# The two experts' weights of a routed feed-forward layer: an exponential and a reciprocal in place of a hyperbolic tangent

## The chip, the cores and the metric

The kernel runs on one core of one Trainium2 chip. The metric is the device time of one execution in microseconds (us).

The core has five engines with queues of their own: TensorE (PE in the profile, with its weight loads as PEld), VectorE (DVE), ScalarE (ACT), GpSimd (POOL) and SyncE (SP). Each runs its instructions in program order and waits on semaphores where it needs another's result.

## The reference, cut to what matters

The input is `x` of 16 images with 64 channels and 32 x 32 pixels. First comes a block of two binary convolutions on the channel-normalised input; its output is added to `x`. Then each of the 16384 pixels is a token of 64 values, which goes through a layer of 16 experts of which it uses two:

```python
logits = jnp.einsum('bsd,de->bse', x, gate_w) + gate_b
probs = jax.nn.softmax(logits, axis=-1)
top_probs, top_idx = jax.lax.top_k(probs, 2)
top_probs = top_probs / jnp.sum(top_probs, axis=-1, keepdims=True)
dispatch = jnp.sum(jax.nn.one_hot(top_idx, n_experts, dtype=x.dtype) * top_probs[..., None], axis=-2)
...
hidden = jax.nn.silu(h1) * h2
expert_out = jnp.einsum('bseh,eho->bseo', hidden, w3)
return jnp.einsum('bseo,bse->bso', expert_out, dispatch)
```

Only the two largest logits enter the two weights. With g as their difference, the weights are (1 + tanh(g/2))/2 for the first expert and (1 - tanh(g/2))/2 for the second.

## The kernel before

**Two halves.** The first half (to about 216 us of the profiled span) computes the convolutions and the routing; the second half computes the experts page by page.

**First half.** The images are taken in 8 pairs, so that 2 x 64 channels fill 128 partitions and a pair has 16 tiles of 128 tokens. All engines run one software pipeline over steps t = 0 to 11. In step t, pair t is normalised, pair t - 1 goes through its convolutions, pair t - 2 is normalised once more and gets its gate logits, pair t - 3 has its two experts chosen, and pair t - 4 gets its weights and the addresses of its rows. Each engine's order within a step is written out by hand:

- ScalarE (L640 to L677): `square2` and `copy2` of pair t - 2; `root(1)`, the logarithm and exponential for that pair's reciprocal root of the variance (L561 to L569); `conv1`; `sign`, `square` and `copy` of pair t; `channels`; `chosen_copy`; `relu`; `root(0)` of pair t; `wide`, which writes `rstd_wide`; `gap_tangent`, the tanh of half the gap (L621 to L625); in steps 3 and 4 a conversion of weights (`make_hi`).
- VectorE (L1458 to L1516): `weights` of pair t - 4 (L1293 to L1299); `first_choice`; `slots`, the rows' addresses; `second_choice`, which also makes the gap and, between its own instructions, `newton_sum` of pair t - 2 (L1189); `channels`; `score`; `places`; `conv2`; `residual`; the first root's steps; `find_line`; `line_parts`; `x_norm`. In step 8 the order of pages follows, in step 11 the list of experts of each page and then `rows_low`, which writes `xs_lo` (L1450).
- TensorE (L838 to L899): `variance(1)` of pair t - 2, for which it needs ScalarE's `square2` (L773); the first convolution; `turn_channels`; `center`; `gate` of pair t - 2 (L802), for which it needs VectorE's `newton_sum`; the second convolution (both at L757); `turn_chosen` (L811); `variance(0)`; `count`; `center2`; `norm` (L785), for which it needs `rstd_wide`; `rank` (L825 to L829).
- GpSimd scatters each pair's rows into pages by an indirect DMA for each tile, once `slots` of the pair is done.

**ScalarE's tables.** A function of ScalarE runs from a set of tables that is loaded by an instruction of its own (ACT_TABLE_LOAD in the profile). The code asks for the set that it names `natural_log_exp_and_others` at the start (L528) and in every `root(1)` (L563); where a function is not in the set that is loaded, a load appears ahead of it under that function's line, as at the tanh (L625) and the first silu (L691).

**The gap and the weights.** `gap` is 128 partitions x 16 tiles of float32. ScalarE waits for `gap_ready`, and from the second pair on for `weights_placed`, so that VectorE has read the last pair's values. VectorE's `weights` waits for `gap_done`. It holds the four experts of each token's line as +1, -1 or 0 in `by_x`, adds the tanh and multiplies by `by_x`: 1 + tanh, 1 - tanh or 0 goes into the row's payload; a factor of two is taken care of at the end. `then(...)` lets an instruction count up a semaphore (`route_link`), and `settled()` waits until all that was counted is done.

**Second half.** TensorE multiplies 147 pages of 128 rows by the weights of four experts each, with the silu on ScalarE, the products on VectorE and the results' scatter on GpSimd; at the end the results are turned back and added to the input.

Of the kernel before, what the change touches and what calls it, by code (L numbers as in the profile page):

```python
# [5 lines left out]
ALU = mybir.AluOpType  # L6
# [9 lines left out]
P = 128  # L16
# [12 lines left out]
PER_LINE = 4  # L29
# [21 lines left out]
def metaformer_kernel(nc, x, w1, gamma1, beta1, mean1, var1, w2, gamma2, beta2, mean2, var2,  # L51
# [33 lines left out]
    with ExitStack() as ctx:  # L85
        def sb(name, shape, dt):
            return ctx.enter_context(nc.sbuf_tensor(name, shape, dt))
# [79 lines left out]
        pick2 = sb("pick2", [P, TILES, E], F32)  # L167
        best = sb("best", [P, 4, TILES], F32)
        gap = sb("gap", [P, TILES], F32)
        gap_tanh = sb("gap_tanh", [P, TILES], F32)  # L170
        chosen = sb("chosen", [P, TILES, E], BF16)
        by_x = sb("by_x", [P, TILES, PER_LINE], F32)
# [353 lines left out]
        def _(act):  # L526
# [32 lines left out]


            def root(n, q):  # L561
                if n == 1:
                    act.preload_act_table_set("natural_log_exp_and_others")  # L563
                act.wait_ge((var_ready, var2_ready)[n], q + 1)
                if q:
                    act.wait_ge((rstd_ready, rstd2_ready)[n], q)
                act.activation(log_var[:, n, :], var_ps[n], ACT.Ln, bias=both_eps[:, n:n + 1]).then_inc(log_made[n], 1)
                act.wait_ge(log_made[n], q + 1)
                act.activation(guess[:, n, :], log_var[:, n, :], ACT.Exp, scale=-0.5).then_inc(guessed[n], 1)  # L569
# [51 lines left out]
            def gap_tangent(q):  # L621
                act.wait_ge(gap_ready, q + 1)
                if q:
                    act.wait_ge(weights_placed, q)
                act.activation(gap_tanh[:, :], gap[:, :], ACT.Tanh, scale=0.5).then_inc(gap_done, 1)  # L625

            def chosen_copy(q):
                act.wait_ge(chosen_turned, q + 1)
# [356 lines left out]
        def _(dve):  # L985
# [161 lines left out]
            def then(ins):  # L1147
                nonlocal links
                links += 1
                ins.then_inc(route_link, 1)  # L1150

            def settled(back=0):
                dve.wait_ge(route_link, links - back)
# [138 lines left out]

            def weights(q):  # L1293
                dve.wait_ge(gap_done, q + 1)
                settled()
                then(dve.tensor_tensor(sided[:, :, :], by_x[:, :, :], spread(gap_tanh[:, :], PER_LINE), ALU.add))
                settled()
                dve.tensor_tensor(payload[q % PAYLOADS][:, :, AT_WEIGHT:AT_WEIGHT + PER_LINE], sided[:, :, :],
                                  by_x[:, :, :], ALU.mult).then_inc(weights_placed, 1)  # L1299
# [304 lines left out]
```

## Time and profile before

| | |
|---|---|
| median of 3 runs | 535.71 us (534.81 to 540.6) |
| profiled execution | 537.69 us, span of the profile 536.0 us |
| mean granted TensorE clock | 0.932 of full speed |
| busy of the span: PE, DVE, ACT, POOL | 88%, 74%, 48%, 53% |
| instructions: DVE, ACT | 913, 462 |

The profile shows one execution. An engine's busy share is an average over both halves; which engine sets the time of a stretch is read from the chain of work that ended last, which is followed back from the last instruction: at each step to what released it, or to the instruction before it on its engine. The granted clock is what TensorE was given of its full 2.4 GHz; 0.50 is its level of 1.2 GHz.

### The profile page before, as it was taken

To read this page: it belongs to the slowest core of one execution; us is meant where nothing else is said; L and a number is where in the kernel's file an instruction comes from. 1 tells how busy PE (TensorE), PEld (TensorE's weight loads), DVE (VectorE), ACT (ScalarE), POOL (GpSimd) and SP (SyncE) were. 2 spreads that over 40 slices of the span, in tenths; PEclk is the share of its full clock that TensorE was granted. 3 is DMA by queue.
4 is the path that set the end of the run, shared out by engine and by line. 5 is a ranking of instruction groups with operands and counts; after the bars stand their busy time and mean duration, and the time that the engine had idled before them with its cause. 6 is when DMAs were issued, how large, how long until landed. Compare 5 with 4: busy or idle time off the path is not lost.

```text
span 536.0 us, 15131 instructions
## 1 busy us (share of the span) xinstructions
PE 474.1 (88%) x4774; PEld 417.1 (78%) x4774; DVE 397.3 (74%) x913; ACT 258.5 (48%) x462; POOL 281.5 (53%) x378
## 2 busy tenths in 40 slices
PE   6889999899998245899999999999999999999991
PEld 5457676767776223899999999999999999999981
DVE  5547777888989988777777677777778777777772
ACT  4557778988777212343443434343433434334320
POOL 4000006777777777777776444444544445455552
PEclk9779879999989756899999999999999999999996
DMA  7981011122000014431233222232422525310234
GB/s 265 325 149 40 1 41 35 53 71 65 30 32 30 28 32 92 87 71 30 62 81 68 56 43 54 49 93 50 121 64 49 130 48 149 75 37 16 74 109 157
DMA packets 62664, 41.03 MB, mean 77 GB/s; under 512 B 50003, under 2 KB 54318, under 8 KB 62080
## 3 DMA queue, kind: packets, MB, share of 16 engines
q1 hardware_dynamic: 52208, 23.84, 19.9%
q0 software_dynamic: 8800, 8.94, 5.2%
q10 hardware_dynamic: 1584, 7.29, 3.4%
q8 instruction: 45, 0.74, 0.6%
q14 instruction: 27, 0.22, 0.1%
HBM read 21.46 MB, written 19.19 MB: 76 GB/s over the span
## 4 chain that ended last, share of the span: by engine, by line
PE 78%; DVE 9%; issue 4%; DMA 3%; ACT 3%; SPq 1%; POOL 0%; POOLq 0%; DVEq 0%; ACTq 0%
PE turn L943 27%; PE up L928 12%; PE up L929 12%; PE up L757 8%; PE small L773 4%; PE small L906 3%; PE small L802 3%; DMA x_in<-in_x 3%; PE up L732 2%; PE turn L785 2%; PE lines L829 1%; PE up L743 1%; PE turn L796 1%; PE lines L950 1%; ACT rstd_wide L576 1%
## 5 line engine op out<-in xcount | busy, mean ns | idle before, releaser
L519 POOL DMA_INDIRECT results<-result,page_in x147 | 145.2, 988 | 129.7 <-ACT xc L691 102.4
L498 POOL DMA_INDIRECT pages<-payload,slot_int x128 | 130.4, 1018 | 108.6 <-DVE slot_int L1351 70.2
L691 ACT ACTIVATE xc<-up,gate_unscale 128x512 f32<-128x512 f32 x147 | 101.1, 687 | 175.5 <-PE up L929 143.6
L928 PE MATMUL up<-xs_hi,up_w 128*128 128x128 f16 x1176 | 148.7, 220 | 3.5 <-DVE hidden L1523 2.0
L929 PE MATMUL up<-xs_lo,up_w 128*128 128x128 f16 x1176 | 148.7, 220 | 0.0
L928 PEld LDWEIGHTS up<-xs_hi,up_w 128*128 x1176 | 123.4, 105 | 4.7 <-issue 4.0
L929 PEld LDWEIGHTS up<-xs_lo,up_w 128*128 x1176 | 115.7, 98 | 0.0
L1523 DVE SCALAR_TENSOR_TENSOR hidden<-up,hidden_scale,xc 128x512 f32<-128x512 f32 x74 | 55.4, 750 | 41.0 <-ACT xc L691 41.0
L943 PE MATMUL turn<-down_raw,hidden 128*128 x592 | 77.7, 275 | 3.4 <-issue 1.7
L943 PE MATMUL turn<-down_raw,sq 128*128 x584 | 78.1, 277 | 2.5 <-issue 0.7
L943 PEld LDWEIGHTS turn<-down_raw,sq 128*128 128x128 f32 x584 | 70.8, 191 | 10.3 <-issue 7.9
L943 PEld LDWEIGHTS turn<-down_raw,hidden 128*128 128x128 f32 x592 | 72.1, 192 | 8.4 <-issue 8.2
L1523 DVE SCALAR_TENSOR_TENSOR sq<-up,hidden_scale,xc 128x512 f32<-128x512 f32 x73 | 54.6, 748 | 24.0 <-ACT xc L691 22.9
L757 PE MATMUL up<-sign,conv_w 128*128 128x512 bf16 x192 | 48.9, 408 | 0.0
L757 PEld LDWEIGHTS up<-sign,conv_w 128*128 128x128 bf16 x192 | 19.8, 108 | 22.5 <-issue 4.7
L773 PE MATMUL small<-mean_col,sq 128*128 128x2 f32 x256 | 31.1, 252 | 5.8 <-ACT sq L553 3.4
L773 PEld LDWEIGHTS small<-mean_col,sq 128*128 128x128 f32 x256 | 30.5, 195 | 6.8 <-issue 3.5
L1534 DVE TENSOR_TENSOR branch<-turn,page_in 128x512 f32<-128x512 f32 (+1 forms) x38 | 25.9, 683 | 6.7 <-PE turn L943 6.6
L1534 DVE TENSOR_TENSOR rstd_wide<-turn,page_in 128x512 f32<-128x512 f32 x36 | 24.9, 691 | 4.7 <-PE turn L943 4.7
L684 ACT ACTIVATE xs_hi<-small 128x512 f16<-128x512 f32 (+1 forms) x37 | 22.0, 594 | 12.2 <-PE small L906 11.8
L1450 DVE SCALAR_TENSOR_TENSOR xs_lo<-small,xs_hi 128x512 f16<-128x512 f32 (+1 forms) x37 | 25.1, 678 | 0.9 <-ACT xs_hi L684 0.9
L802 PE MATMUL small<-gate_mat,xc 128*128 128x32 f32 x128 | 16.8, 288 | 9.9 <-DVE slack L1189 9.9
(234 smaller groups left out, 618.2 us busy)
## 6 DMA issues: line engine op xcount, KB each, us to landing
pages<-x ACTq DMA_DIRECT2D x4, 1332.0 KB, 10.8
page_in<-pages SPq DMA_DIRECT2D x147, 36.0 KB
page_in<-pages SPq DMA_DIRECT2D x147, 32.0 KB
x_in<-in_x SPq DMA_DIRECT2D x7, 512.0 KB, 3.5
out<-up_raw SPq DMA_DIRECT2D x5, 512.0 KB, 3.1
results<-result,page_in POOLq DMA_INDIRECT x147
up_raw<-in_L_ffn_w SPq DMA_DIRECT2D x4, 512.0 KB, 17.6
pages<-payload,slot_int POOLq DMA_INDIRECT x128
```

Source lines behind the costliest of these rows:

```text
L498: pool.indirect_dma_start(out=pages, out_offset=bass.IndirectOffsetOnAxis(ap=slot_int[q % PAYLOADS][:, t:t + 1], axis=0), in_=payload[q % ...
L519: pool.indirect_dma_start(out=results, out_offset=bass.IndirectOffsetOnAxis(ap=page_in[g % LOADS][:, k, D + AT_TOKEN:D + AT_TOKEN + 1].bit ...
L691: act.activation(act_s[n % 2], up[n % 2][:, 0:CW], ACT.Silu, scale=gate_unscale[:, 0:1])\
L757: last = pe.matmul(cv[c], conv_w[:, which, t, :], image[:, c * ROWS + i:(c + 1) * ROWS + i, j:j + W], start=(t == 0), stop=(t == len(TAPS) ...
L773: last = pe.matmul(var_ps[n][:, 2 * j:2 * j + 2], sq[:, j * P:(j + 1) * P], mean_col[:, :], start=True, stop=True)
L802: last = pe.matmul(gate_ps[:, j * 2 * E:(j + 1) * 2 * E], xc2[:, j * P:(j + 1) * P], gate_mat[:, :, :].rearrange("p a e -> p (a e)"), star ...
L928: pe.matmul(target, own, xs_hi[g % 2][:, at], start=True, stop=False)
L929: last = pe.matmul(target, own, xs_lo[g % 2][:, at], start=False, stop=True)
L943: last = pe.matmul(target, hidden[n % RING][:, at], whole[:, bass.ds(e, D)], start=True, stop=True)
L1450: dve.scalar_tensor_tensor(out=xs_lo[g % 2][:, 0:width], in0=small[:, 0:width], scalar=X_SCALE, in1=xs_hi[g % 2][:, 0:width], op0=ALU.mult ...
L1523: dve.scalar_tensor_tensor(out=hidden[n % RING], in0=up[n % 2][:, CW:HW], scalar=hidden_scale[:, 0:1], in1=act_s[n % 2], op0=ALU.mult, op1 ...
L1534: dve.tensor_tensor(weighed[g % 2][:, k:k + count, :, :], down_pair(m)[:, 0:count, :, :], weights.unsqueeze(3).to_broadcast([P, count, PER ...
```

## The change

With e = exp(-g), tanh(g/2) = (1 - e)/(1 + e). ScalarE computes e; VectorE adds 1, takes the reciprocal, and multiplies it by e - 1, which gives the negative of the tanh; the addition to `by_x` becomes a subtraction. There are two new tiles of 128 x 16 float32, the call for the table set in `root(1)` is dropped, and in `weights` the wait `settled()` ahead of the first instruction is dropped, with one behind each new instruction.

```diff
@@ -167,6 +167,8 @@
         gap = sb("gap", [P, TILES], F32)
+        gap_exp = sb("gap_exp", [P, TILES], F32)
+        gap_part = sb("gap_part", [P, TILES], F32)
         gap_tanh = sb("gap_tanh", [P, TILES], F32)
@@ -559,8 +561,6 @@
             def root(n, q):
-                if n == 1:
-                    act.preload_act_table_set("natural_log_exp_and_others")
                 act.wait_ge((var_ready, var2_ready)[n], q + 1)
@@ -622,7 +622,7 @@
                 act.wait_ge(gap_ready, q + 1)
                 if q:
                     act.wait_ge(weights_placed, q)
-                act.activation(gap_tanh[:, :], gap[:, :], ACT.Tanh, scale=0.5).then_inc(gap_done, 1)
+                act.activation(gap_exp[:, :], gap[:, :], ACT.Exp, scale=-1.0).then_inc(gap_done, 1)
@@ -1292,8 +1292,14 @@
             def weights(q):
                 dve.wait_ge(gap_done, q + 1)
-                settled()
-                then(dve.tensor_tensor(sided[:, :, :], by_x[:, :, :], spread(gap_tanh[:, :], PER_LINE), ALU.add))
+                then(dve.tensor_scalar(gap_part[:, :], gap_exp[:, :], 1.0, None, ALU.add))
+                settled()
+                then(dve.reciprocal(gap_part[:, :], gap_part[:, :]))
+                settled()
+                then(dve.scalar_tensor_tensor(out=gap_tanh[:, :], in0=gap_exp[:, :], scalar=-1.0, in1=gap_part[:, :],
+                                              op0=ALU.add, op1=ALU.mult))
+                settled()
+                then(dve.tensor_tensor(sided[:, :, :], by_x[:, :, :], spread(gap_tanh[:, :], PER_LINE), ALU.subtract))
                 settled()
```

## Rows read from the trace of the kernel before

**Rows 1.** The page's chain that ended last: share of the span by engine

```profile
PE 78%; DVE 9%; issue 4%; DMA 3%; ACT 3%; SPq 1%; POOL 0%; POOLq 0%; DVEq 0%; ACTq 0%
```

**Rows 2.** ScalarE's groups of instructions: line, operation, tile, count, busy us, mean ns

```profile
L563 ACT ACT_TABLE_LOAD x8 | 10.3, 1283 | 0.1
...
L625 ACT ACT_TABLE_LOAD x7 | 9.0, 1283 | 0.1
...
L625 ACT ACTIVATE gap_tanh<-gap 128x16 f32<-128x16 f32 x8 | 1.7, 215 | 0.1
```

**Rows 3.** ScalarE's timeline, 0 to 36 us: start, duration, line, operation, tile

```profile
1.24 1.28 ACT L528 ACT_TABLE_LOAD   x1 [1.24 <-PEq L1593]
...
13.80 0.27 ACT L567 ACTIVATE log_var<-small,both_eps 128x16 f32<-128x16 f32 x1 [1.69 <-PE small L773]
14.11 0.22 ACT L569 ACTIVATE guess<-log_var 128x16 f32<-128x16 f32 x1
...
34.97 1.28 ACT L563 ACT_TABLE_LOAD   x1
```

**Rows 4.** The chain in order of time, 93 to 98 us: start, duration

```profile
93.47 1.28 ACT L625
...
96.77 1.07 ACT sq L602 x2
```

**Rows 5.** TensorE's timeline, rounds 5 to 7; in brackets the idle time before it

```profile
95.15 1.34 PE L829 MATMUL lines<-line_hot,ones_b 128*128 128x320 bf16 x16
97.89 1.95 PE L773 MATMUL small<-mean_col,sq 128*128 128x2 f32 x16 [1.40 <-ACT sq L602]
...
104.94 1.87 PE L802 MATMUL small<-gate_mat,xc 128*128 128x32 f32 x16
...
116.83 1.93 PE L773 MATMUL small<-mean_col,sq 128*128 128x2 f32 x16
...
123.86 1.87 PE L802 MATMUL small<-gate_mat,xc 128*128 128x32 f32 x16
...
144.11 1.87 PE L802 MATMUL small<-gate_mat,xc 128*128 128x32 f32 x16
```

**Rows 6.** VectorE's groups of instructions, small shapes

```profile
L1194 DVE SCALAR_TENSOR_TENSOR rstd<-slack,guess 128x16 f32<-128x16 f32 x16 | 2.8, 173 | 0.3
...
L1122 DVE RECIPROCAL scales<-largest 128x3 f32<-128x3 f32 x1 | 0.2, 177 | 0.0
...
L1134 DVE RECIPROCAL unscale<-unscale 128x1 f32<-128x1 f32 x1 | 0.2, 165 | 0.0
```

**Rows 7.** VectorE timeline: a reciprocal, its successor, newton_sum in rounds 5 to 7

```profile
53.91 0.18 DVE L1122 RECIPROCAL scales<-largest 128x3 f32<-128x3 f32 x1
54.12 0.17 DVE L1123 TENSOR_SCALAR scales<-scales 128x3 f32<-128x3 f32 x1
...
102.89 0.17 DVE L1189 SCALAR_TENSOR_TENSOR slack<-small,slack 128x16 f32<-128x16 f32 x1
...
123.37 0.17 DVE L1189 SCALAR_TENSOR_TENSOR slack<-small,slack 128x16 f32<-128x16 f32 x1
...
142.87 0.17 DVE L1189 SCALAR_TENSOR_TENSOR slack<-small,slack 128x16 f32<-128x16 f32 x1
```

**Rows 8.** The chain in order of time, rounds 8 and 9

```profile
155.26 0.23 DVE sided L1296
...
163.45 1.97 PE small L802 x16
165.42 2.64 PE up L757 x12
...
177.41 0.24 DVE sided L1296
```

**Rows 9.** VectorE timeline at the first page of the second half; brackets: idle

```profile
211.02 0.69 DVE L1450 SCALAR_TENSOR_TENSOR xs_lo<-small,xs_hi 128x512 f16<-128x512 f32 x1 [0.92 <-ACT xs_hi L684]
```

**Rows 10.** Two us by engine: PE, PEld, DVE, ACT, POOL, granted clock, DMA, GB/s

```profile
132.00:134.00 2.00, 1.61 (x8) 1.61 (x9) 0.53 (x2) 1.98 (x3) 1.70 (x2) 0.50 0.74 270
```

## The prediction

> **What bounds the kernel now.** I read the chain that ended last first: TensorE carries 78% of the span, VectorE 9%, ScalarE 3% [rows 1]. The change touches only the first half (up to about 216 us), in the loop of steps t = 0 to 11 that I call rounds, so the question is which engine that chain runs through where ScalarE's table loads and VectorE's `weights` stand. I therefore read ScalarE's groups, to see what is removed; the chain around the one load that lies on it; TensorE's and VectorE's timelines of rounds 5 to 7; and the chain of rounds 8 to 11. The reader is to see three stretches. Up to round 7 the chain is TensorE's own work, and ScalarE makes it wait for a load once, in round 5 [rows 4, 5]. From `weights` of round 8 on, VectorE is the chain: `sided` stands on it in rounds 8 and 9 [rows 8], and so it goes on in round 10. In round 11 VectorE waits again, for ScalarE's `xs_hi` [rows 9]. Behind that the second half is TensorE's and is not touched, so a delay of the first half moves its end by the same amount.
>
> **What the change removes.** Fifteen table loads of 1283 ns: 8 asked for in `root` and 7 placed before the tanh, 19.2 us of ScalarE's time in all [rows 2]. No pause hangs on them: the idle time ahead of the 8 tanh is 0.1 us together [rows 2]. The exponential takes the place of the tanh at the same price: 0.22 us for the same shape, against 215 ns [rows 2, 3]. That no new load appears is read from the start: the table loaded at 1.24 us serves a logarithm at 13.80 and an exponential at 14.11, and the next load comes at 34.97 and is asked for by the code [rows 3]. So one set has all that the loop needs once the tanh is gone. The load for the silu stays.
>
> What of the 19.2 us lies on the chain? In 14 of 15 cases ScalarE catches up before TensorE needs it. In round 6, for instance, TensorE starts `variance` at 116.83 with no idle time ahead of it [rows 5], although two loads lie around it. These 14 I cost at nothing; TensorE's own matmuls are the cover. The exception is round 5. TensorE ends `rank` at 95.15 + 1.34 = 96.49 and waits until 97.89 for ScalarE's squares, which end at 96.77 + 1.07 = 97.84 behind the load of 93.47 and a weight conversion [rows 4, 5]. Without the load the squares end at 96.56 and TensorE starts at about 96.61: **-1.28 us**, bounded from below by nothing and from above by the wait of 1.40.
>
> [...]
>
> **What it adds.** Three VectorE instructions in each `weights`, in a chain of dependences. An add and a scalar_tensor_tensor of 128x16: 173 ns each by the nearest row [rows 6]. A reciprocal of 128x16 is not in the trace: 165 ns at one column and 177 at three [rows 6] make 165 as the lower bound and, at 6 ns a column, 165 + 15 x 6 = 255 as the upper; I take 210. From the end of one to a dependent start goes 0.03 us (53.91 + 0.18 to 54.12) [rows 7]. Together 0.20 + 0.24 + 0.20, so **0.65 us** a round, 0.60 to 0.70.
>
> [...]
>
> Behind `weights` on VectorE stand the choice of experts, `slots`, and `newton_sum`, for which TensorE's `gate` (L802) waits. Round by round:
> - Round 4 is covered by the clock-slowed TensorE work that VectorE waits for; I cost it at nothing, and at 0.65 if that cover is gone.
> - Round 5: `newton_sum` ends at 103.06 [rows 7], with the addition 103.71. `gate` would start at 104.94 - 1.28 = 103.66 [rows 5]. **+0.1**: the gain of 1.28 just fits.
> - Round 6: `newton_sum` ends at 123.54, with the addition 124.19, but TensorE was ready at 123.86 [rows 5, 7]. **+0.35**: here TensorE waits anew, and all behind `gate` is later.
> - Round 7: 143.04 + 0.65 = 143.69 before 144.11 [rows 5, 7]: nothing, because TensorE had lost time at its lower clock just before [rows 10]. At full clock it would cost as in round 6.
> - Rounds 8, 9 and 10: on the chain [rows 8], nothing covers it: 3 x 0.65 = **+1.95**.
> - Round 11: the wait of 0.92 us ahead of `xs_lo` [rows 9] swallows it.
>
> **Sum:** -1.28 + 0.1 + 0.35 + 1.95 = +1.1 us. The profiled execution took 537.69 us (span 536.0), 2 us above the median of the runs; the change is small against both, so I add it to the median: 535.71 + 1.1 = **536.8 us**. The bounds of the prices: lowest -1.40 + 0 + 0.2 + 1.8 = +0.6; highest, with no gain in round 5, rounds 4, 6 and 7 uncovered and 0.70 each, 0.7 x 6 = +4.2, and that is 539.9.
>
> **Rivals.**
> - *The table loads are on the path throughout.* [...] If each of the 15 loads delayed the chain, their removal would give 15 x 1.283 = 19.2 us, against 1.95 to 4.2 added: about 519 to 520. For it: ScalarE loses these 19.2 us for certain. Against it: ScalarE is 3% of the chain, and one load stands on it [rows 1, 4]. Chance 0.05.
> - *The lower clock reaches round 8* (ends on the other side). TensorE's granted clock drops to 0.50, the 1.2 GHz level, in places: in 132 to 134 us, where TensorE was busy 1.61 of 2.00 us [rows 10]. The addition makes TensorE wait longer for `newton_sum` ahead of `gate` of round 8. If the clock falls there, `gate` and the convolution behind it, 1.97 + 2.64 = 4.6 us on the chain [rows 8], take twice as long: 536.8 + 4.6 = 541.4. It decides only if the whole stretch is slow. For it: such a drop already followed a partly idle stretch. Against it: VectorE's chain, not TensorE's clock, sets rounds 9 to 11. Chance 0.09.
> - *VectorE binds in every round.* Six or seven rounds at 0.65 and no gain: 539.6 to 540.3. Against it: the covers counted above. Chance 0.06.
> - *The change doesn't do what it says:* logarithm and exponential get different sets and each `root` pays two loads. For the 8 roots on the chain that is 8 x 2 x 1.283 = 20.5 us: 557. Against it: rows 3 show both under one load. Chance 0.02.
>
> **How the numbers follow.** The forecast, with the clock's drops moved by at most a stretch either way, has 0.78. Such a stretch of some 3 us at half speed costs about 1.5 us, estimated from the halved clock [rows 10]; two less or two more of them make 536.8 -/+ 3. With the bound of 539.9 and the case of VectorE in every round, the range is 533.5 to 540.5. A measurement of this kernel tells about 1%, 5.4 us, from no change. Faster by more than that needs the first rival: 0.05. Slower needs the clock, the wrong sets, or both costs together: 0.11. Within 1%: 0.84.
>
> **What would show it.** Right: one table load at the start and one before the first silu, 19 us less busy time on ScalarE, no idle TensorE ahead of round 5's `variance`, an idle TensorE of some 0.3 us ahead of round 6's `gate`, `weights` longer by 0.65 us, and the first `xs_lo` about 1 us later. Wrong: further table loads; a reciprocal much above 255 ns; `xs_lo` earlier than 211.02; another count of stretches at the lower clock; or a second half that is not as long as before.

## The result and the profile after

| | before | after |
|---|---|---|
| median | 538.22 us (20 runs, 534.52 to 544.54) | 540.66 us (20 runs, 537.9 to 543.78) |
| profiled execution, span | 537.69 us, 536.0 us | 539.03 us, 537.3 us |
| mean granted TensorE clock | 0.932 | 0.932 |

The ratio after to before is 1.0049 [1.0028, 1.0070], so +2.6 us [+1.5, +3.8]. (Ratios leave disturbed executions out, so they need not be the quotient of two medians.) The 20 runs of before also put its median 2.5 us above the 535.71 us of the three runs that the prediction started from. 540.66 us lies 3.9 us above the forecast of 536.8 and 0.16 us above the range.

The page of after, first the busy time of the engines (share of the span, instructions), then the chain that ended last. VectorE has 11% of the chain where before it had 9% [rows 1]:

```profile
PE 475.3 (88%) x4774; PEld 416.6 (78%) x4774; DVE 402.0 (75%) x937; ACT 238.9 (44%) x447; POOL 279.8 (52%) x378
...
PE 82%; DVE 11%; issue 3%; ACT 2%; DMA 1%; POOL 1%; POOLq 0%; DVEq 0%; SPq 0%
```

ScalarE's groups of after (line, operation, tile, count, busy us, mean ns). Of the fifteen loads of [rows 2] none is left; the load at the start and the one for the silu stay. The exponential takes 201 ns where the tanh took 215:

```profile
L625 ACT ACTIVATE gap_exp<-gap 128x16 f32<-128x16 f32 x8 | 1.6, 201 | 0.0
L530 ACT ACT_TABLE_LOAD x1 | 1.3, 1283 | 1.3 <-PEq L1599 1.3
L691 ACT ACT_TABLE_LOAD x1 | 1.3, 1283 | 0.0
```

VectorE's groups of the three new instructions, and its timeline where they run in round 4 (start, duration). From the start of the first to the start of `sided` it is 91.74 - 91.05 = 0.69 us:

```profile
L1297 DVE RECIPROCAL gap_part<-gap_part 128x16 f32<-128x16 f32 x8 | 2.0, 253 | 0.3
...
L1299 DVE SCALAR_TENSOR_TENSOR gap_tanh<-gap_exp,gap_part 128x16 f32<-128x16 f32 x8 | 1.4, 174 | 0.3
...
L1295 DVE TENSOR_SCALAR gap_part<-gap_exp 128x16 f32<-128x16 f32 x8 | 1.3, 166 | 0.0
```

```profile
91.05 0.16 DVE L1295 TENSOR_SCALAR gap_part<-gap_exp 128x16 f32<-128x16 f32 x1
91.24 0.25 DVE L1297 RECIPROCAL gap_part<-gap_part 128x16 f32<-128x16 f32 x1
91.53 0.17 DVE L1299 SCALAR_TENSOR_TENSOR gap_tanh<-gap_exp,gap_part 128x16 f32<-128x16 f32 x1
91.74 0.23 DVE L1302 TENSOR_TENSOR sided<-by_x,gap_tanh 128x64 f32<-128x64 f32 x1
```

So what the change does to the two engines is what was predicted. The time went elsewhere, and TensorE's timeline shows where. After, round 4 to round 5: the wait of 1.40 us ahead of `variance` [rows 5] is gone (93.36 has no bracket), but behind the wait for `rstd_wide` the `norm` takes 1.97 us and the four products behind it 1.84:

```profile
88.43 1.97 PE L785 MATMUL turn<-ident,rstd_wide 128*128 128x128 f32 x8 [0.91 <-ACT rstd_wide L576]
90.19 1.84 PE L743 MATMUL up<-x,center_mat 128*128 128x256 f32 x4
...
93.36 1.93 PE L773 MATMUL small<-mean_col,sq 128*128 128x2 f32 x16
```

The same place in round 5 of before, with the same wait, at full clock:

```profile
113.47 1.18 PE L785 MATMUL turn<-ident,rstd_wide 128*128 128x128 f32 x8 [0.91 <-ACT rstd_wide L576]
114.48 1.03 PE L743 MATMUL up<-x,center_mat 128*128 128x256 f32 x4
```

Four stretches of after around that `norm` in rounds 4 to 7 (us, busy time by engine, then the granted clock, here 0.57 to 0.73; 0.50 in 109 to 111 us alone):

```profile
88.00:92.00 4.00, 3.57 (x13) 3.02 (x14) 2.23 (x8) 3.37 (x5) 3.06 (x4) 0.57 0.44 154
108.00:112.00 4.00, 3.09 (x13) 2.81 (x13) 2.25 (x7) 1.74 (x4) 3.09 (x4) 0.61 0.54 168
128.00:132.00 4.00, 3.09 (x13) 2.52 (x12) 2.30 (x7) 1.74 (x4) 2.95 (x4) 0.67 0.50 162
148.00:152.00 4.00, 3.10 (x13) 2.62 (x14) 2.54 (x10) 1.97 (x6) 3.08 (x4) 0.73 0.10 31
```

After's rounds are 20.48 us long there, from each `norm` to the next; before, where the `norm` ran at full clock in rounds 4 and 5 (1.18 us), the round from 113.47 to 132.39 took 18.92.

And in round 8, TensorE's timeline of after: the gate waits 1.16 us for `newton_sum`, and the convolution behind it takes 4.46 us, where in before the same twelve products took 2.81 us (2.64 on the chain, [rows 8]) behind a wait of 0.54 (granted clock 0.51 in 164 to 167 us of after, 1.00 in 165.4 to 168 us of before):

```profile
161.42 1.97 PE L802 MATMUL small<-gate_mat,xc 128*128 128x32 f32 x16 [1.16 <-DVE slack L1189]
163.23 4.46 PE L757 MATMUL up<-sign,conv_w 128*128 128x512 bf16 x12
```

Put together for the two profiled executions, each mark's start in us:

| mark | before | after | difference |
|---|---|---|---|
| `norm` of round 3 | 71.17 | 69.11 | -2.06 |
| `norm` of round 4 | 92.98 | 88.43 | -4.55 |
| `norm` of round 5 | 113.47 | 108.92 | -4.55 |
| `norm` of round 7 | 152.64 | 149.88 | -2.76 |
| `gate` of round 8 | 163.45 | 161.42 | -2.03 |
| `gate` of round 9 | 185.61 | 185.89 | +0.28 |
| first `xs_lo` | 211.02 | 211.99 | +0.97 |

The first -2.06 is not the change's: it was there at `gate` of round 2 (42.73 against 40.69), because before's `norm` at 29.95 ran at the lower clock (1.97 us, where after's at 29.27 took 1.17), ahead of the first load that the change removes (34.97, [rows 3]). The `xs_lo` row of after answers to [rows 9]; its wait for ScalarE has shrunk from 0.92 to 0.43 us:

```profile
211.99 0.69 DVE L1456 SCALAR_TENSOR_TENSOR xs_lo<-small,xs_hi 128x512 f16<-128x512 f32 x1 [0.43 <-ACT xs_hi L684]
```

From the first `hidden` to the end of the span both take about the same: 536.0 - 215.78 = 320.2 and 537.3 - 216.75 = 320.6 us. So the first `xs_lo` came 1 us later, as predicted, but out of other terms. Between rounds 3 and 4 after gained 2.5 us, where before ran at the lower clock; its stretch behind the `norm` of round 3 (the granted clock is the 0.50 behind the engines):

```profile
72.00:76.00 4.00, 4.00 (x16) 2.87 (x15) 3.35 (x9) 3.99 (x6) 0.00 (x0) 0.50 0.13 49
```

Between rounds 4 and 5 it gained nothing: the wait of 1.40 us is gone and the slow stretch behind `norm` took its place. By round 7 it gave back 1.8 us, and from there to `xs_lo` it lost 0.73 + 2.31 + 0.69 = 3.7 us instead of 1.95.

### The profile page after: what moved, and what is told of

It is laid out like the page before. It is cut to its first block, busy times and chain, and to the rows that moved or that the text cites. A ratio compares the mean times of both kernels' runs of the same rounds, so it can differ in the third digit from the quotient of the medians.

```text
span 537.3 us, 15132 instructions
## 1 busy us (share of the span) xinstructions
PE 475.3 (88%) x4774; PEld 416.6 (78%) x4774; DVE 402.0 (75%) x937; ACT 238.9 (44%) x447; POOL 279.8 (52%) x378
## 4 chain that ended last, share of the span: by engine, by line
PE 82%; DVE 11%; issue 3%; ACT 2%; DMA 1%; POOL 1%; POOLq 0%; DVEq 0%; SPq 0%
PE turn L943 27%; PE up L928 12%; PE up L929 12%; PE up L757 9%; PE small L773 5%; PE small L906 3%; PE small L802 3%; PE up L732 3%; PE turn L785 2%; PE lines L829 1%; PE up L743 1%; PE turn L796 1%; PE lines L950 1%; ACT rstd_wide L576 1%; DVE up_w L1142 1%
## 5 line engine op out<-in xcount | busy, mean ns | idle before, releaser
L500 POOL DMA_INDIRECT pages<-payload,slot_int x128 | 128.6, 1005 | 109.7 <-DVE slot_int L1357 68.1
L757 PE MATMUL up<-sign,conv_w 128*128 128x512 bf16 x192 | 51.4, 423 | 0.0
L757 PEld LDWEIGHTS up<-sign,conv_w 128*128 128x128 bf16 x192 | 20.5, 112 | 24.6 <-issue 8.6
L684 ACT ACTIVATE xs_hi<-small 128x512 f16<-128x512 f32 (+1 forms) x37 | 22.0, 594 | 12.1 <-PE small L906 11.8
L802 PEld LDWEIGHTS small<-gate_mat,xc 128*128 128x128 f32 x128 | 16.9, 209 | 12.3 <-DVE slack L1189 12.1
```

The lines of the kernel that those rows point to most:

```text
L500: pool.indirect_dma_start(out=pages, out_offset=bass.IndirectOffsetOnAxis(ap=slot_int[q % PAYLOADS][:, t:t + 1], axis=0), in_=payload[q % ...
L684: act.activation(xs_hi[g % 2][:, 0:width], small[:, 0:width], ACT.Copy, scale=X_SCALE)\
L757: last = pe.matmul(cv[c], conv_w[:, which, t, :], image[:, c * ROWS + i:(c + 1) * ROWS + i, j:j + W], start=(t == 0), stop=(t == len(TAPS) ...
L802: last = pe.matmul(gate_ps[:, j * 2 * E:(j + 1) * 2 * E], xc2[:, j * P:(j + 1) * P], gate_mat[:, :, :].rearrange("p a e -> p (a e)"), star ...
```

## The experiments

Two theories went in. P: the prices of the prediction, the lower clock comes by chance. C: TensorE's waits, which the change moves, decide where its clock falls. Changes in us are the ratio times the median of before in the same set (539.55, then 541.25, then 539.22).

### The loads alone

`loads_only` is the changed kernel without its three VectorE instructions:

```diff
-                then(dve.tensor_scalar(gap_part[:, :], gap_exp[:, :], 1.0, None, ALU.add))
-                settled()
-                then(dve.reciprocal(gap_part[:, :], gap_part[:, :]))
-                settled()
-                then(dve.scalar_tensor_tensor(out=gap_tanh[:, :], in0=gap_exp[:, :], scalar=-1.0, in1=gap_part[:, :],
-                                              op0=ALU.add, op1=ALU.mult))
-                settled()
-                then(dve.tensor_tensor(sided[:, :, :], by_x[:, :, :], spread(gap_tanh[:, :], PER_LINE), ALU.subtract))
+                settled()
+                then(dve.tensor_tensor(sided[:, :, :], by_x[:, :, :], spread(gap_exp[:, :], PER_LINE), ALU.subtract))
```

> The changed kernel without its three new VectorE instructions: the exponential goes into the weights as it is, so the weights are wrong ones and only the time is of use. What is left of the change is that 15 table loads are gone. Theory P (the terms of the prediction's sum hold, and the stretches of TensorE's lower clock move about by chance): -1.3 us against the kernel before, 0.24% faster. Theory C (without the loads, rounds 5 to 8 each have a stretch at the lower clock and take 20.5 us, so what the loads gave back is lost there): no gain, 0 to +1.5 us, and the profile shows a stretch at 1.2 GHz behind the wait for rstd_wide in all four rounds.

Measured: 537.21 us, ratio 0.9941 [0.9903, 0.9979], -3.2 us. The gain is larger than the one load of 1.28 us that P found on the chain, but its interval, -5.2 to -1.1 us, just reaches that. C was wrong on the time. Its mechanism is in the profile, though: the `norm` of rounds 5, 6 and 7 takes 1.97 us (at 111.40, 131.54 and 151.86; the granted clock was 0.50 in 111.4 to 113.4 us), that of round 4 1.18. This execution took 537.45 us, about as long as the profiled one of before (537.69), so the two profiles don't show where the 3.2 us come from.

### The three instructions alone

`trio_only` is the kernel before, with its tanh and its loads, and three instructions of the same shapes whose result nobody reads:

```diff
-                settled()
+                then(dve.tensor_scalar(gap_part[:, :], gap_tanh[:, :], 3.0, None, ALU.add))
+                settled()
+                then(dve.reciprocal(gap_part[:, :], gap_part[:, :]))
+                settled()
+                then(dve.scalar_tensor_tensor(out=gap_exp[:, :], in0=gap_tanh[:, :], scalar=-1.0, in1=gap_part[:, :],
+                                              op0=ALU.add, op1=ALU.mult))
+                settled()
                 then(dve.tensor_tensor(sided[:, :, :], by_x[:, :, :], spread(gap_tanh[:, :], PER_LINE), ALU.add))
```

> The kernel before with its tanh and all its table loads, and three VectorE instructions of the same kinds and shapes as the new ones ahead of sided in weights; their result is used by nothing. Theory P: +2.3 us (0.35 in round 6, 3 x 0.65 in rounds 8 to 10), 0.43% slower; with the loads' -1.3 this makes the +1.0 of the sum. Theory C: the same +2.3 us, and it is nearly all that the whole change costs (+2.6). If the three instructions cost more than their durations say, +3.5 us or more.

Measured: 540.98 us, ratio 1.0047 [1.0004, 1.0091], +2.5 us [+0.2, +4.9]. The size is as both theories expected. TensorE's timeline shows two things: in round 6 the gate waits 0.26 us for `newton_sum`, as the prediction had for that round (+0.35), and at 143.10 in round 7 again; and in round 8 the wait of 1.12 us is again followed by a convolution of 4.46 us:

```profile
123.65 1.97 PE L804 MATMUL small<-gate_mat,xc 128*128 128x32 f32 x16 [0.26 <-DVE slack L1191]
...
163.22 1.97 PE L804 MATMUL small<-gate_mat,xc 128*128 128x32 f32 x16 [1.12 <-DVE slack L1191]
165.03 4.46 PE L759 MATMUL up<-sign,conv_w 128*128 128x512 bf16 x12
```

### The three instructions from round 8 on

`trio_late` runs them only where the prediction has them on the chain:

```diff
+                if q >= 4:
                     then(dve.tensor_scalar(gap_part[:, :], gap_exp[:, :], 1.0, None, ALU.add))
 ...
+                else:
+                    settled()
+                    then(dve.tensor_tensor(sided[:, :, :], by_x[:, :, :], spread(gap_exp[:, :], PER_LINE), ALU.subtract))
```

> The changed kernel with its three new VectorE instructions in the last four of the eight pairs only (rounds 8 to 11); in the first four the exponential goes into the weights as it is, so half of the weights are wrong ones. Theory P: -1.3 + 1.95 = +0.7 us. Theory C: +1.95 to +3.5 us, the same as the whole change, since rounds 4 to 7 cost nothing by either account but for 0.35.

Measured: 539.11 us, ratio 1.0003 [0.9970, 1.0037], +0.2 us. Against before that is nearer to P's number than to C's, but the gain from the loads, which P had put at 1.3 us and C at nothing, had come out larger than either. Against `loads_only`, which differs by these four rounds alone, it is +3.4 us by the ratios and 1.9 us by the two medians (539.11 and 537.21), so the times don't decide between 1.95 us and more. The two profiles, which both have the `norm` of round 7 at the lower clock, show more: `norm` of round 7 to `gate` of round 8 is 11.49 against 10.82 us, that gate to the next 24.44 against 22.10, and on to `xs_lo` 26.10 against 25.40: 0.67 + 2.34 + 0.70 = 3.7 us, as from before to after. In `loads_only` the gate of round 8 waits 0.52 us and the convolution stays at full clock (1.00 in 164.5 to 167 us):

```profile
162.68 1.97 PE L802 MATMUL small<-gate_mat,xc 128*128 128x32 f32 x16 [0.52 <-DVE slack L1189]
164.49 2.81 PE L757 MATMUL up<-sign,conv_w 128*128 128x512 bf16 x12
```

So in these profiles the three instructions cost about 0.7 us in each of these rounds, and in round 8 1.6 us more by TensorE's clock.

### No loads and nothing more on VectorE

tanh(g/2) = 2/(1 + e) - 1, and 1/(1 + e) = exp(-ln(1 + e)). The one table load at the start serves both the logarithm and the exponential [rows 3], so `on_scalar` lets ScalarE compute the whole and folds the factors into the two VectorE instructions that are there anyway:

```diff
-                act.activation(gap_exp[:, :], gap[:, :], ACT.Exp, scale=-1.0).then_inc(gap_done, 1)
+                act.activation(gap_exp[:, :], gap[:, :], ACT.Exp, scale=-1.0).then_inc(gap_step, 1)
+                act.wait_ge(gap_step, 2 * q + 1)
+                act.activation(gap_log[:, :], gap_exp[:, :], ACT.Ln, bias=all_one[:, 0:1]).then_inc(gap_step, 1)
+                act.wait_ge(gap_step, 2 * q + 2)
+                act.activation(gap_tanh[:, :], gap_log[:, :], ACT.Exp, scale=-1.0).then_inc(gap_done, 1)
@@ weights
+                then(dve.scalar_tensor_tensor(out=sided[:, :, :], in0=spread(gap_tanh[:, :], PER_LINE), scalar=2.0,
+                                              in1=by_x[:, :, :], op0=ALU.mult, op1=ALU.add))
+                settled()
+                dve.scalar_tensor_tensor(out=payload[q % PAYLOADS][:, :, AT_WEIGHT:AT_WEIGHT + PER_LINE],
+                                         in0=sided[:, :, :], scalar=-1.0, in1=by_x[:, :, :],
+                                         op0=ALU.add, op1=ALU.mult).then_inc(weights_placed, 1)
```

> All on ScalarE, in the one table set that stays: e = exp(-g), then ln(1 + e), then exp of the negative of that, which is the first expert's weight; VectorE's weights has two instructions as before the change, of another kind. ScalarE's table loads are gone and 0.55 us a round are added to it. Theory P: -0.8 to -1.3 us against the kernel before. Theory C: 0 to +1.5 us. Both: 2.3 us less than the changed kernel or a little more.

Measured: 535.37 us, ratio 0.9939 [0.9908, 0.9969], -3.3 us: faster than before. ScalarE's groups show the price, 0.72 us a round where the tanh took 0.22:

```profile
L627 ACT ACTIVATE gap_log<-gap_exp,all_one 128x16 f32<-128x16 f32 x8 | 2.5, 308 | 0.3
L629 ACT ACTIVATE gap_tanh<-gap_log 128x16 f32<-128x16 f32 x8 | 1.7, 216 | 0.2
L625 ACT ACTIVATE gap_exp<-gap 128x16 f32<-128x16 f32 x8 | 1.6, 200 | 0.0
```

In its profile the `norm` of rounds 4 to 7 runs at full clock each time (1.18 us), and from round 5 on the rounds are 18.92 us long. But ScalarE has little room in the two rounds in which it also converts weights. TensorE waits 0.56 us for its squares in rounds 4 and 5; in round 4 the clock falls behind that wait (0.59 in 80 to 83 us), and from `norm` to `norm` it is 94.68 - 73.39 = 21.29 us:

```profile
77.46 2.15 PE L777 MATMUL small<-mean_col,sq 128*128 128x2 f32 x16 [0.56 <-ACT sq L602]
79.47 4.24 PE L761 MATMUL up<-sign,conv_w 128*128 128x512 bf16 x12
```

And the gate of round 8 waits 1.24 us, and the clock falls there too (0.57 in 164 to 168 us):

```profile
162.25 1.97 PE L806 MATMUL small<-gate_mat,xc 128*128 128x32 f32 x16 [1.24 <-DVE slack L1193]
164.05 4.46 PE L761 MATMUL up<-sign,conv_w 128*128 128x512 bf16 x12
```

### TensorE kept busy in the wait for `rstd_wide`

`after_again` is the changed kernel once more. `after_fill`, `before_fill` and `on_scalar_fill` are the changed kernel, the kernel before and `on_scalar`, each with four products that nobody reads in the wait ahead of the first half of `norm`, in rounds 1 to 7:

```diff
-                pe.wait_ge(widened, CH * q + c + 1)
                 if q == 1:
 ...
+                if q and c == 0:
+                    for _ in range(4):
+                        pe.matmul(turn[0][:, :], ident_b[:, :],
+                                  conv_w[:, 0, 0:4, :].rearrange("p t o -> p (t o)"), start=True, stop=True)
+                pe.wait_ge(widened, CH * q + c + 1)
                 for t in range(TPC):
```

> The changed kernel once more, unaltered, on the same chip as the three kernels with filled waits. By all theories +1.1 to +2.6 us against the kernel before; theory C adds that its profile again has a stretch at 1.2 GHz behind the wait for rstd_wide in most of rounds 4 to 8 and that its mean granted clock is lower than that of the kernel before.

> The changed kernel with four matrix products of 128x512 in bf16 in TensorE's wait for rstd_wide (0.91 us a round), into a bank that the transposes behind them overwrite; nothing reads their result. Theory C (the changed kernel loses 1 us and more a round to stretches at 1.2 GHz that begin behind that wait): with the wait filled TensorE keeps 2.4 GHz, rounds 5 to 7 take 19.2 to 19.5 us in place of 20.5, and the kernel is 3 to 4 us faster than the changed kernel, so 0.5 to 2 us faster than the kernel before. Theory P (the stretches come by chance, and not from that wait): as the changed kernel, within 0.5 us.

> The kernel before with the same four products in the same wait. Theory C: 2 to 4 us faster than the kernel before, which has two such stretches in rounds 7 and 8 of its profile at 1.3 to 1.5 us each. Compared with the changed kernel that has its wait filled, the difference is then what the prediction's sum says without the clock: 1.1 us. Theory P: as the kernel before.

> The kernel with all three functions on ScalarE (on_scalar), and the same four products in the same wait. Its profile without them has no stretch at 1.2 GHz in rounds 4 to 8, so both theories expect little: theory C 0 to 1.5 us less than on_scalar, since other executions of it have such stretches; theory P the same as on_scalar, 3 to 4 us below the kernel before.

| | median, us | ratio to before | us |
|---|---|---|---|
| `after_again` | 540.15 | 0.9994 [0.9965, 1.0023] | -0.3 |
| `after_fill` | 533.18 | 0.9878 [0.9821, 0.9936] | -6.6 |
| `before_fill` | 535.12 | 0.9880 [0.9824, 0.9937] | -6.5 |
| `on_scalar_fill` | 535.08 | 0.9893 [0.9844, 0.9942] | -5.8 |

In the changed kernel and in the kernel before, this is the largest effect of a single edit in the study, and it comes from work that computes nothing; it is more than C had forecast (3 to 4 and 2 to 4 us). `on_scalar` gains less by it: its ratio was 0.9939 without the products and is 0.9893 with them, in another set, and the medians are alike (535.37 and 535.08). With the wait filled the three ways to compute the weights can't be told apart: their changes lie within 0.8 us, each with some 3 us either side. TensorE's timeline of `after_fill`, round 5: the four products take 1.03 us where TensorE waited 0.91, `norm` runs in 1.24 us instead of 1.97, and from round 4 to round 7 each round takes 19.33 us instead of 20.48:

```profile
108.15 1.03 PE L784 MATMUL turn<-conv_w,ident_b 128*128 128x512 bf16 x4
109.22 1.24 PE L789 MATMUL turn<-ident,rstd_wide 128*128 128x128 f32 x8
110.30 1.03 PE L743 MATMUL up<-x,center_mat 128*128 128x256 f32 x4
```

With this cover gone, the next place shows: the gate of round 8 now waits 1.92 us, and the clock falls behind it as before the fill (0.54 in 161 to 164 us):

```profile
158.68 1.97 PE L806 MATMUL small<-gate_mat,xc 128*128 128x32 f32 x16 [1.92 <-DVE slack L1193]
160.49 4.45 PE L757 MATMUL up<-sign,conv_w 128*128 128x512 bf16 x12
```

`before_fill` shows what went with a table load on the chain. Its profiled execution is one of its two longest (540.7 us; the other four took 532.5 to 536.6 at mean granted clocks of 0.938 to 0.947 against 0.930, and where their clock fell isn't seen). ScalarE's timeline, and under it TensorE's: the load of 69.62 and the conversion `up_w` stand ahead of the squares; TensorE waits 1.34 us for them, and behind the wait `variance` takes 2.86 us and the convolution 5.16, against 1.93 and 2.80 in before (77.42 and 79.21); the granted clock was 0.50 in 77 to 81 us. That is 1.34 + 0.93 + 2.36 = 4.6 us, in round 4 (the wait at 74.04) and once more behind the wait of 1.33 us at 97.80:

```profile
69.62 1.28 ACT L625 ACT_TABLE_LOAD   x1
70.91 0.22 ACT L625 ACTIVATE gap_tanh<-gap 128x16 f32<-128x16 f32 x1
71.03 1.99 ACT L636 ACTIVATE up_w<-up_raw,scales 128x2048 f16<-128x2048 f32 x1
72.93 1.06 ACT L602 ACTIVATE sq<-up 128x512 f32<-128x512 f32 x2
```

```profile
71.36 1.34 PE L833 MATMUL lines<-line_hot,ones_b 128*128 128x320 bf16 x16
74.04 2.86 PE L773 MATMUL small<-mean_col,sq 128*128 128x2 f32 x16 [1.34 <-ACT sq L602]
76.77 5.16 PE L757 MATMUL up<-sign,conv_w 128*128 128x512 bf16 x12
```

So in this one execution a load of 1.28 us goes with a loss of 4.6 us, where the clock falls behind the wait. Where it doesn't, the loss stays near the wait, as in round 5 of before [rows 5] and in `before_hold`, one of the kernels below. That has the same two waits, at full clock (1.00 in 72 to 100 us); its rounds with them are 20.49 us long each (`norm` at 66.95, 87.44 and 107.93), the two behind them 18.98 and 18.99 (126.91 and 145.90), so a load is worth 1.5 us there:

```profile
71.85 1.95 PE L773 MATMUL small<-mean_col,sq 128*128 128x2 f32 x16 [1.33 <-ACT sq L602]
...
92.34 1.95 PE L773 MATMUL small<-mean_col,sq 128*128 128x2 f32 x16 [1.34 <-ACT sq L602]
```

### TensorE kept busy ahead of round 8, and in rounds 9 and 10

`after_gate8` is the changed kernel with five products only ahead of the gate of round 8. The three `_hold` kernels are the three `_fill` kernels with these five, and with 40 more in the long waits ahead of the gate of round 9 and ahead of `turn_chosen` of round 10:

```diff
+                if q == PAIRS - 2:
+                    fill(up[0][:, 0:CW], 5)
+                if q == PAIRS - 1:
+                    fill(up[0][:, 0:CW], 40)
                 pe.wait_ge(var2_read, q + 1)
@@ turn_chosen
+                if q == PAIRS - 1:
+                    fill(up[0][:, 0:CW], 40)
                 pe.wait_ge(chosen_ready, q + 1)
```

> The changed kernel with five matrix products of 128x512 in bf16 at one place only: TensorE's wait for newton_sum ahead of gate of round 8 (1.1 to 1.2 us in the changed kernel), into a bank that is free by then; nothing reads their result. Theory C (the longer wait there lets the clock fall in the convolution behind it, which took 4.46 us in place of 2.81): the convolution takes 2.8 us again and the kernel is 1.6 us faster than the changed kernel. Theory P: the products lie in a wait and change nothing, within 0.5 us.

> The changed kernel with products in all of TensorE's long waits of the first half from round 1 on: four ahead of norm, five ahead of gate of round 8, forty ahead of gate of round 9 and forty ahead of turn_chosen of round 10, so that TensorE keeps 2.4 GHz. Theory C: the kernel with only the wait ahead of norm filled, less 1.6 us in round 8, 1.8 us at gate of round 9 (3.62 to 1.87) and some 2 us at rank and the first page's transposes: 5 us less than that one, 11 to 12 us less than the changed kernel. Theory P: as the changed kernel.

> The kernel before with the same products in the same waits. Theory C: 9 to 12 us less than the kernel before; its rounds 4 and 5 keep TensorE's wait for the squares behind a table load and, in some executions, a lower clock behind that. With the clock held, the terms of the prediction's sum give 0.3 to 1.1 us less than the changed kernel with the same products; if the loads let the clock fall in rounds 4 and 5, it is slower than that one by up to 5 us.

> The three functions on ScalarE and the same products in the same waits. Theory C: the fastest of all: 2.5 to 3.5 us less than the changed kernel with the same products (0.34 a round in rounds 5 to 8, 0.65 in rounds 9 and 10), 13 to 15 us less than the kernel before. Theory P: as on_scalar.

| | median, us | ratio to before | us |
|---|---|---|---|
| `after_gate8` | 539.41 | 1.0020 [0.9991, 1.0050] | +1.1 |
| `after_hold` | 532.88 | 0.9879 [0.9824, 0.9935] | -6.5 |
| `before_hold` | 534.98 | 0.9901 [0.9849, 0.9953] | -5.3 |
| `on_scalar_hold` | 529.71 | 0.9840 [0.9782, 0.9898] | -8.6 |

In its own place `after_gate8` does what it is for: TensorE's timeline of round 8 has no wait and the convolution at full clock (1.00 in 165.8 to 168.5 us).

```profile
162.89 1.03 PE L801 MATMUL up<-conv_w,ident_b 128*128 128x512 bf16 x4
164.00 1.97 PE L809 MATMUL small<-gate_mat,xc 128*128 128x32 f32 x16
165.81 2.81 PE L757 MATMUL up<-sign,conv_w 128*128 128x512 bf16 x12
```

With it the wait of round 8 can be set against the length of that stretch in eight profiles without a fill at `norm`:

| kernel | idle ahead of the gate | convolution behind it | gate of round 8 to gate of round 9 |
|---|---|---|---|
| `loads_only` | 0.52 | 2.81 | 22.10 |
| before | 0.54 | 2.81 | 22.16 |
| `after_gate8` | 0, filled | 2.81 | 22.85 |
| `on_scalar` | 1.24 | 4.46 | 23.76 |
| `trio_late` | 1.10 | 4.46 | 24.44 |
| `trio_only` | 1.12 | 4.46 | 24.47 |
| `after_again` | 1.13 | 4.46 | 24.47 |
| after | 1.16 | 4.46 | 24.47 |

The two costs come apart: with the three instructions the stretch is 24.47 - 23.76 = 0.71 us longer at the same clock, and with the fall of the clock 24.47 - 22.85 = 1.62 us longer with the same instructions. In this place the wait of 1.1 us and more comes with the fall each time, the waits of 0.52 and 0.54 us and the filled one don't. That is no rule for other places: in `on_scalar` the fall came behind the wait of 0.56 us ahead of the squares.

The time of the whole kernel doesn't show these 1.6 us: +1.1 us against before, where `after_again` had -0.3 in another set, with intervals that overlap. In the profile of `after_gate8` the `norm` of rounds 1 and 2 ran at the lower clock (at 50.09 for 1.97 us, where after has 1.18) and its `norm` of round 7 starts at 152.46, 2.6 us later than after's. Why its early rounds are slower than after's is left open.

`after_hold` brings the gate of round 9 back to full clock, 1.97 us for 3.62 in after (1.00 in 181.6 to 183.6 us, where after has 0.50 in 185.9 to 189.5), and shows no `norm` above 1.24 us from round 1 on:

```profile
171.62 8.58 PE L805 MATMUL up<-conv_w,ident_b 128*128 128x512 bf16 x39
181.64 1.97 PE L815 MATMUL small<-gate_mat,xc 128*128 128x32 f32 x16 [1.44 <-DVE slack L1204]
```

From gate to gate it is 181.64 - 158.80 = 22.84 us, and the first `hidden` starts at 210.38, 3.8 us earlier than in `after_fill`. In the medians of six runs each that isn't seen: 532.88 against 533.18. `on_scalar_hold` is the fastest kernel, 8.6 us below before [5.5, 11.8]; in its profile the first `hidden` starts at 204.50, against 215.78 in before. C had asked for more of all three: 11 to 12 us below the changed kernel, where `after_hold` is 6.5 us below `after_gate8` in the same set, and 9 to 12 and 13 to 15 us below before, where `before_hold` and `on_scalar_hold` have 5.3 and 8.6.

## Why the prediction missed

**In short.** Of the 3.9 us above the forecast, 2.5 are the base (535.71 us, where 20 runs have a median of 538.22), and the rest is the change, +2.6 us where the sum had +1.1. The step of the sum that failed is the price of a wait of TensorE: it was set at the wait's own length, and the lower clock that can follow was left out of the sum, as a rival in round 8 and as chance elsewhere. In rounds 8 to 10, where the prediction had 3 x 0.65 = 1.95 us, the profiles show 3.7, of which 1.65 are the clock's in round 8.

**Loads removed: right.** Fifteen loads are gone, no other came, ScalarE is busy 19.6 us less. The rival that had each of them on the path (519 to 520 us) fell: without the three instructions, `loads_only` gained 3.2 of 19.2 us. The other 16.0 us didn't show in the time; in round 6 of before, for instance, TensorE starts `variance` at 116.83 with no wait [rows 5], with loads at 113.95 and 117.42. No pause shows at a load: in `before_fill` the tanh starts at 70.91, right behind the load that ended at 69.62 + 1.28 = 70.90, and in before ScalarE was idle for 0.1 us together ahead of the seven loads at the tanh, and for 0.1 us ahead of the eight tanh [rows 2].

**The term of -1.28 was read from one execution.** The prediction found the one load on the chain, priced it at its own length with the wait of 1.40 us as the upper bound, and cost the other 14 at nothing, with TensorE's own matmuls as the cover. Measured alone, the loads were worth -3.2 us [-5.2, -1.1], which isn't clear of -1.28. Two steps are too short. One of the 14, the load of round 4, was covered in before's profile by the lower clock alone (72 to 76 us); in `before_hold`, at full clock, TensorE waits 1.33 us for it, and the two rounds are 1.5 us longer each, 3.0 us together. And the wait is no upper bound: in the profile of `before_fill` a wait of 1.34 us was followed by 3.3 us lost at the lower clock. How often either happens in before isn't shown: its profiled execution has one such wait, at full clock.

**The price of the three instructions: right,** at the upper end. The reciprocal took 253 ns, where the rows gave 165 to 255 (the 255 an estimate at 6 ns a column) and the prediction took 210; the three together 0.69 us, and 0.71 by the table of round 8, against 0.65 (0.60 to 0.70).

**Rounds 5 to 7: right in mechanism, hidden by the clock.** The predicted idle TensorE ahead of round 6's `gate` isn't there after (120.87 has no bracket): TensorE had lost more than that at the lower clock in the `norm` of round 5 (1.97 us for 1.18), as the prediction had argued for round 7 alone. Where the clock stayed up, in `trio_only` (`norm` of rounds 5 and 6 in 1.18 us), the gate waited 0.26 us in round 6 and 0.26 in round 7. With the wait filled the whole round tells the same: 19.33 us from `norm` to `norm` in `after_fill` and `after_hold`, against 18.98 in rounds 6 and 7 of `before_hold`, so 0.35 us, the price that the prediction had for round 6.

**Rounds 8 to 10: the term of +1.95 was mis-sized, at 3.7 us.** VectorE is the chain there, as predicted, and 0.73 + 0.66 + 0.69 of it are the three instructions (the middle one is 2.31 less the clock's 1.65). The rest is the rival of the lower clock in round 8, which had a chance of 0.09 and a price of 4.6 us. It came, by the mechanism that the prediction named, the longer wait for `newton_sum` ahead of the gate. It took the convolution alone (4.46 against 2.81 us) and left the gate at 1.97, so its price was 1.65. The argument against it, that VectorE's chain sets these rounds, failed: what VectorE does next waits for that convolution. Its timeline shows it idle for 0.55 and 1.22 us ahead of the two halves of `residual` in after (L1166, at 165.75 and 167.72), each time for TensorE's L757, and for 0 and 0.21 us in before. The sum of 3.7 us is that of two pairs of profiles (before and after, `loads_only` and `trio_late`); the medians don't confirm it by themselves.

**The clock in rounds 4 to 7 was left out of the sum.** The prediction let its stretches move by one "either way" and so gave them a mean of nothing. After has one in the `norm` of every round from 4 to 7; `after_again`, `after_gate8` and `trio_late` have the same four, `loads_only` has three of them, before two, `trio_only` one, `on_scalar` none. They cost 20.48 - 19.33 = 1.15 us a round against `after_fill`, and 4 x 1.15 = 4.6 of the 6.3 us that the fill is worth against `after_again` (-6.6 against -0.3). That they hang on TensorE's wait for `rstd_wide` is shown by the fill: with it the `norm` took 1.24 us in each of rounds 1 to 7. Why the same wait of 0.91 us was followed by the fall in all of rounds 4 to 7 of after and in none of them in `on_scalar` isn't settled.

**With the clock held.** From the `norm` of round 3 to the first `xs_lo` the profile of `before_hold` takes 200.97 - 66.95 = 134.02 us and that of `after_hold` 205.63 - 70.65 = 134.98; the mean granted clock was 0.97 in 67 to 200 us of the one and 0.99 in 70 to 205 us of the other. So with every `norm` and `gate` there at full clock the change costs 0.96 us, where the prediction's sum has 1.1. The terms differ: -2.3 us in rounds 4 and 5, +0.7 in rounds 6 and 7, +2.6 from there on. The medians of the two kernels (534.98 and 532.88 us) don't resolve a microsecond.

**Small sums of large terms.** In the two profiles of before and after `xs_lo` was 0.97 us later, and the prediction said about 1. That is luck, since the terms that make it up are not the ones forecast. Set out by cause it was -3.2 for the loads and +3.7 for rounds 8 to 10, with the clock of rounds 4 to 7 on top, in which before has two falls in one execution and after four. So the size of the whole change isn't sharp: +2.6 us [+1.5, +3.8] in the first set, -0.3 [-1.9, +1.2] in another, where the changed kernel kept its time (540.66 and 540.15) and before did not (538.22 and 541.25). Faster by 1% or slower by 1% it was in neither.

**The base.** 535.71 us was the median of three runs, with one of them at 540.6; the profiled execution took 537.69. The prediction took the lower of the two for its base. From the profiled execution the same sum would have given 538.8, from the median of the 20 runs 539.3, both within the range and with the same errors in the terms.

## What to carry to other kernels

Where TensorE was the chain here, a stall of its feeding engine did not always end with its own length: behind a wait of 1.40 us the clock stayed at 1.00 in before, one of 1.34 us went with a loss of 4.6 us in `before_fill`. Look at what the granted clock does behind each of TensorE's waits, and price a wait with and without a stretch at the lower clock behind it. A wait of about a microsecond that comes back in each round may be worth filling with products that nobody reads; four of them a round gave 1.2% here, in the changed kernel and in the kernel before, more than the change to the tables did. And a small chain of dependent steps may be better placed on an engine off the chain than on the one that is the chain: the same weights from two exponentials and a logarithm on ScalarE made the kernel 0.6% faster instead of 0.5% slower. With all of TensorE's long waits filled it was 1.6%, against 1.2% for the changed kernel and 1.0% for the kernel before, with intervals that overlap; with one wait filled no difference is seen. Room is a matter of the round: where ScalarE also converts weights, TensorE waited for it (0.56 us in `on_scalar`).

## What the runs showed of the hardware

- TensorE's granted clock was 0.50 in 72 to 76 us of before, in 109 to 111 us of after and in 77 to 81 us of `before_fill`, and 1.00 in 113.5 to 117.5 us of before and in 72 to 100 us of `before_hold`. The profile prints these shares and no frequency. At 1.00, in `after_hold`, three products of 512 columns took 0.81 us and 39 took 8.58, so 0.216 us for each one more; at 0.50, in 77 to 81 us of `before_fill`, 0.43 us each (twelve in 5.16 us). That is an estimated 2.4 and 1.2 columns a ns, and if a column is taken as a cycle, the 2.4 and 1.2 GHz of the texts on record.
- The same wait of 0.91 us was followed by a `norm` of 1.97 us (clock 0.57 to 0.73 over 4 us) in some rounds and of 1.18 us (clock 1.00) in others. In round 8 waits of 1.10 to 1.92 us were followed by the fall (a convolution of 4.31 to 4.46 us) in all eight profiles that have one with no fill there (five of the table above and the three `_fill` kernels), waits of 0.52 and 0.54 us in neither of two (2.81 us). Ahead of the squares, waits of 0.50 to 0.56 us were followed by a convolution of 4.24 to 4.45 us in one of two such rounds in each of `on_scalar`, `on_scalar_fill` and `on_scalar_hold`, and waits of 1.33 to 1.40 us by one of 2.80 to 2.81 us in before, `trio_only` and `before_hold`, but of 5.16 and 5.28 us in `before_fill`. The length of the wait alone doesn't tell.
- In the profiles of after, `after_again`, `after_gate8` and `trio_late` the fall came back in the same place in each of rounds 4 to 7, with a `norm` of 1.97 us and rounds of 20.3 to 20.5 us; with the wait filled (`after_fill`) it came in none, with a `norm` of 1.24 us and rounds of 19.33.
- The time of before went with its mean granted clock from one execution to the next: its 35 executions in the first set of experiments run from 534.9 us at 0.935 to 546.3 us at 0.918, with a correlation of -0.90.
- In after a reciprocal of 128 x 16 took 253 ns on VectorE, against 166 and 174 ns for an addition and a scalar_tensor_tensor of the same shape.
